# Score matmuls of a cross attention on 128 rows instead of 97 and 98, in a one-core decoder layer

## The reference, cut to what matters

```python
x = x + L0_attn(layernorm(x), ...)              # two Mamba-2 scans, forward and backward
x = x + L0_xattn(layernorm(x), ctx, ctx, ...)   # the part that is changed
x = x + L0_ffn(layernorm(x), ...)               # attention over a mixture of experts

def L0_xattn(q, k, v, padding_mask, ...):       # B, S, D = 4, 1024, 512; 16 heads of HD = 32
    Q, K, V = q @ W_q.T + b_q, k @ W_k.T + b_k, v @ W_v.T + b_v      # split into heads
    scores = einsum('bhqd,bhkd->bhqk', Q, K) / sqrt(HD)
    scores = where(causal, -inf, scores)                # key later than query
    scores = where(padding_mask, -inf, scores)
    return (softmax(scores) @ V) @ W_o.T + b_o
```

## Time and profile before

| | us |
|---|---|
| median of 3 runs | 7218.32 (7214.54 to 7227.69) |
| the profiled execution | 7219.6 |
| its span, first to last instruction | 7217.7 |
| PE busy | 5176.3 (72%) |
| DVE busy | 3053.4 (42%) |
| ACT busy | 1409.7 (20%) |
| POOL busy | 1340.0 (19%) |

### The profile page before, as it was taken

How to read it: one execution, slowest core, us unless ns; L and a number is a source line. 1 busy time by engine, 2 the same in 40 slices (tenths; PEclk the granted TensorE clock), 3 DMA queues, 4 the chain that set the end, 5 groups by cost and what they waited for, 6 DMA issues and landing times. The chain is left out here.

```text
span 7217.7 us, 76090 instructions
## 1 busy us (share of the span) xinstructions
PE 5176.3 (72%) x25256; PEld 3663.9 (51%) x25256; DVE 3053.4 (42%) x6335; ACT 1409.7 (20%) x3256; POOL 1340.0 (19%) x983
## 2 busy tenths in 40 slices
PE   4776666756666766756667678788787859797978
PEld 3555545545445454555455443444435427576666
DVE  3434434434344444444444443343433435344353
ACT  1221212212111211212112123132231310101000
POOL 1222222212214423423424200000000000000000
PEclk8887888877877877877778778888788879788888
DMA  1000000000100000000000231412313120101000
GB/s 49 11 11 8 8 13 7 11 12 7 55 9 20 23 14 12 29 8 17 24 8 21 83 80 35 122 43 75 80 43 113 43 84 6 36 0 36 9 27 21
DMA packets 114630, 236.68 MB, mean 33 GB/s; under 512 B 20373, under 2 KB 20377, under 8 KB 113177
## 3 DMA queue, kind: packets, MB, share of 16 engines
q1 hardware_dynamic: 114200, 231.23, 10.5%
HBM read 155.15 MB, written 67.11 MB: 31 GB/s over the span
## 5 line engine op out<-in xcount | busy, mean ns | idle before, releaser
L1259 DVE TENSOR_REDUCE xa_mx<-xa_s 128x1 f32<-128x128 f32 (+7 forms) x512 | 374.1, 754 | 477.6 <-PE xa_s L1328 471.4
L1172 ACT ACTIVATE xa_src<-xa_gen 128x512 f32<-128x512 f32 (+3 forms) x768 | 354.9, 490 | 600.4 <-PE xa_gen L1348 394.1
L812 PE MATMUL mb_ib<-mb_wc,mb_yT 128*128 128x512 f32 x512 | 280.0, 709 | 225.6 <-ACT mb_yT L529 225.6
L1327 PE MATMUL xa_s<-xa_ka,xa_qa 97*128 97x512 f32 (+3 forms) x768 | 289.6, 442 | 205.2 <-DVE xa_mx L1259 124.6
L812 PE MATMUL mf_ib<-mf_wc,mf_yT 128*128 128x512 f32 x512 | 268.1, 684 | 205.9 <-ACT mf_yT L529 205.9
L1345 PE MATMUL xa_gen<-xa_qa,xa_ka 98*128 98x512 f32 (+3 forms) x768 | 339.4, 466 | 86.4 <-DMA xa_qa<-xa_rows 43.7
L1135 POOL TENSOR_TENSOR xa_res<-xa_res,xa_bor 128x512 f32<-128x512 f32 x32 | 40.3, 1264 | 1769.8 <-DMA xa_res<-after_mamba_dram 1769.8
L72 PE MATMUL ff_gen<-ff_w_hi,ff_st_hi 128*128 128x512 f32 x768 | 309.3, 403 | 0.0
L73 PE MATMUL ff_gen<-ff_w_hi,ff_st_lo 128*128 128x512 f32 x768 | 306.4, 399 | 0.0
L74 PE MATMUL ff_gen<-ff_w_lo,ff_st_hi 128*128 128x512 f32 x768 | 306.2, 399 | 0.0
L622 DVE SCALAR_TENSOR_TENSOR mb_cv<-mb_xc,mb_cw,mb_cv 128x256 f32<-128x256 f32 x432 | 195.6, 526 | 256.0 <-POOL mb_cv L410 254.8
(11 more groups left out here) (441 smaller groups left out, 12948.5 us busy)
## 6 DMA issues: line engine op xcount, KB each, us to landing
xa_qa<-xa_q_dram SPq DMA_DIRECT2D x192, 128.0 KB, 3.2
xa_ka<-xa_k_dram SPq DMA_DIRECT2D x192, 128.0 KB, 3.4
xa_k_dram<-xa_kq SPq DMA_DIRECT2D x32, 512.0 KB, 2.8
xa_q_dram<-xa_kq SPq DMA_DIRECT2D x32, 512.0 KB, 2.8
ff_src<-after_attn_dram SPq DMA_DIRECT2D x64, 256.0 KB, 2.7
mf_xg<-in_x_dram SPq DMA_DIRECT2D x16, 512.0 KB, 3.7
part_dram<-mf_hb SPq DMA_DIRECT2D x32, 256.0 KB, 2.1
mb_xg<-in_x_dram SPq DMA_DIRECT2D x16, 512.0 KB, 3.8
```

The lines of the kernel that those rows point to most:

```text
L812: last = mm(ps[:], yT[:, k, :], wc[:, k, :], start=k == 0, stop=k == KI - 1)
L1172: a_.activation(pe_x[:, s % 2, hh, 0:w], gen["p2", g, s, hh][:, 0:w], ACT.Exp, scale=XSCALE)\
L1259: v_.tensor_reduce(mx[:, g % 2, i, hh:hh + 1], s1[g, hh, i][:, 0:(i + 1) * P], AX.X, ALU.max)\
L1327: mm(ps[:, a:b], qa[s][0:ROW_MAX, i * P:(i + 1) * P], ka[s][0:ROW_MAX, a:b], start=True, stop=b < n)
```

## The change

Every slot tile gets zeros in partitions 96 to 127 at the start, and a row of zeros (`zrow`, a row of the tile `rows`) is made. Both score matmuls then read all 128 partitions. The first pass must not see the maximum that an earlier head left in partition 97 of `qa`, so each head's load also moves `zrow` there, and PE waits for eight transfers instead of seven. The start values take two steps on DVE, zeros and then ones, `const_dve` counts to 2, and SP waits for it ahead of its loop.

```diff
@@ cross_attention
-        mrow, maskf = rows_[0:HG, :], rows_[XD:XD + 1, :]
+        mrow, maskf, zrow = rows_[0:HG, :], rows_[XD:XD + 1, :], rows_[2 * XD:2 * XD + 1, :]
...
-        rows_loaded = [sig(f"rows_loaded{i}", 7 * XH // SLOTS, 16) for i in range(SLOTS)]
+        rows_loaded = [sig(f"rows_loaded{i}", 8 * XH // SLOTS, 16) for i in range(SLOTS)]
@@ sync
             sp.wait_ge(half_ready, 3)
+            sp.wait_ge(const_dve, 2)
             with sp.Fori(0, B) as it:
@@ sync, load(h)
                     sp.dma_start(ka[s][ROW_MASK:ROW_MASK + 1, :].bitcast(F32), maskf.bitcast(F32))\
                         .then_inc(rows_loaded[s].sem, 16)
+                    sp.dma_start(qa[s][ROW_MAX:ROW_MAX + 1, :].bitcast(F32), zrow.bitcast(F32)).then_inc(rows_loaded[s].sem, 16)
@@ vector
             v_.memset(ones[:], 1.0)
+            v_.memset(zrow.bitcast(F32), 0.0)
+            for t in qa + ka:
+                last = v_.memset(t[ROW_MASK:P, :].bitcast(F32), 0.0)
+            last.then_inc(const_dve, 1)
+            dve.wait_ge(const_dve, 1)
             for t in qa + ka:
                 last = v_.memset(t[ROW_MASK:ROW_MAX + 1, :].bitcast(F32), 1.0)
             last.then_inc(const_dve, 1)
-            dve.wait_ge(const_dve, 1)
+            dve.wait_ge(const_dve, 2)
@@ tensor
-            pe.wait_ge(const_dve, 1)
+            pe.wait_ge(const_dve, 2)
@@ tensor, pass1
-                        pe.wait_ge(rows_loaded[s].sem, rows_loaded[s].at(it, 7 * (h // SLOTS) + 6))
+                        pe.wait_ge(rows_loaded[s].sem, rows_loaded[s].at(it, 8 * (h // SLOTS) + 7))
...
-                        mm(ps[:, a:b], qa[s][0:ROW_MAX, i * P:(i + 1) * P], ka[s][0:ROW_MAX, a:b], start=True, stop=b < n)
+                        mm(ps[:, a:b], qa[s][:, i * P:(i + 1) * P], ka[s][:, a:b], start=True, stop=b < n)
@@ tensor, pass2
-                    last = mm(ps[:, 0:n], ka[sl][0:ROW_MAX + 1, j * P:(j + 1) * P], qa[sl][0:ROW_MAX + 1, a:a + n],
+                    last = mm(ps[:, 0:n], ka[sl][:, j * P:(j + 1) * P], qa[sl][:, a:a + n],
                               start=True, stop=not diagonal)
```

## The result

The changed kernel takes 7244.45 us in the median of 10 runs (7226.51 to 7255.08), the kernel before 7221.48 (7209.33 to 7227.89) beside it. The ratio is 1.0032 with a 95% interval of 1.0022 to 1.0042: slower, by 23 us (16 to 30), which is 0.3%. The forecast was 7236, 18 us slower. Ratios here leave out one execution, of the second pass padded, that took 9336 us at a mean clock of 0.54.

The account below looks back on a forecast made before the run. A chain of PE work and DMA waits in cross attention was taken as the bound, PE full at low clock being lost time. Terms 24 + 14 - 20 = +18 us on 7218.3 gave 7236 us, range 7212 to 7262.

Parts of the forecast that it names:

- Start values: Start of cross attention: 17 memsets, a wait and SP's no longer hidden context load delay PE by 24.1 us, bounds 20 to 36.
- the other two bounds: Time of one wide start memset on DVE if not 0.91 us: 0.72 by partitions times columns, or 1.63 if both added up.
- Zero rows: SP's queue: 64 added 4 KB transfers delay the maxima rows and slot releases, costing 14 us, bounds 8 and 18.
- The clock: Second passes of cross attention: padded score matmuls bring the higher granted clock sooner, gaining 20 us, bounds 0 and 80.
- the eight long stretches: Low clock for about 16 us each after head loads of groups 2 and 3; gain 0.6 us each, 5 us together.
- single ones: Single low-clock stretches with a full PE, worth 1.3 us each; four counted on, 5 us.
- No clock gain: Rival: the grant goes by a busy PE, or by rows holding more than zeros; costs of 38 remain, 7256 us; chance 0.20.
- its second form: Variant of the no clock gain rival: only rows that hold more than zeros count towards the granted clock.
- The clock up throughout: Rival: clock stays up through the second pass, removing 154 us of low clock, worth 62 to 69; about 7190 us; chance 0.10.
- Its condition of 95 us of low clock: Removed low clock from which that rival decides: costs of 38 us divided by a worth of 0.4.
- Weight loads ahead: Rival: padding lets the mask matmul's weight loads start early, up to 0.10 us in 1024 pairs; 7161 us; chance 0.06.
- Costs paid back in full: Rival: zero rows cost only 8 us and the clock gains 32, so no change; chance 0.06.

Follow-up runs that it names:

- three moved lines: Kernel before with only the order changed: group 0's maxima rows issued behind the loads of heads 4 and 5 instead of 4 to 7; ratio 0.9961.

## Why the prediction was right

**Start values** (forecast 24.1): 24.1 in the trace after and in the kernel with these alone. The memset on 32 partitions takes 0.91 us; the other two bounds fall.

**Zero rows** (forecast 14, as 2.3 a batch ahead of the maxima, 1.7 at the slots, less 2): 14.6 by the waits of the kernel with these alone. Ahead of the maxima the step was too small: 11.8 / 4 = 2.95 a batch (in the kernel after PE waits 13.6 us in the mean, where 12 to 13 were named). A row costs SP 0.63 and not 0.57, which makes 2.5 for four, and nothing caught up; the other 0.4 is as much as the two profiles of the kernel before differ. At the slots it was too large, 2.8 us in twelve waits and 1.0 in the kernel after, where 6.8 were counted, and kernels without the row lie between 77.4 and 81.0 there, so even 82.0 is hardly a cost. The DMA issues of the kernel after (count, KB, median us to landing), against the earlier trace rows:

```profile
xa_qa<-xa_rows SPq DMA_DIRECT2D x128, 4.0 KB, 2.4
xa_ka<-xa_rows SPq DMA_DIRECT2D x64, 4.0 KB, 2.8
```

The first line mixes the 64 zero rows (median 2.6 us) with the 64 maxima rows (1.8, as before). The mask row, last of a head load before, landed 3.4 us after its issue; now it takes 2.8, and the zero row, issued 0.55 us later, lands only some 0.3 us after it. That the engines were still busy with the head's data, which a later row then waits for less, fits; no run tests it alone.

**The clock** (forecast 20): 17 by the ratio of the padding alone (10 to 23). That it came so near is partly luck, for two errors cancel. Behind the maxima, 46.1 us of low clock became 23.7, much as forecast (46 to 20). But low clock elsewhere went too: the eight long stretches lost 3.4 us each and one of them 6.8, not 1.5, and single ones vanished. In all 302 us became 221 in the kernel after, 80 less where the steps' terms come to about 50. And a low microsecond was worth less: (256.4 - 251.6) x 4 = 19 us for 80, or 0.24, not 0.4. The zero rows' cost is in that too; the padding alone has (256.4 - 250.5) x 4 = 24 us for 88, or 0.27. The 91% busy stretch behind the maxima, from which I took the worth, isn't typical: over the whole second passes PE is busy for 80% (206.24 of 256.68 us in batch 1). Where the clock now rises inside a long stretch, PE waits for DVE. The first pass standing alone, for which the sum has no term, also lost low clock (29.5 us a batch to 24.7 after, to 22.6 in the padding alone, where it got 0.9 us shorter).

**Sum**: forecast +18, measured +23 (16 to 30). The parts measured alone give 28 + 14 - 17 = 25.

**The rivals.** No clock gain falls by the padding alone; its second form, that zero rows don't count, falls by it too, and the ones do no better. The clock up throughout falls: 55 of 252 us are still at 0.50 in each batch's second passes. Its condition of 95 us of low clock was nearly met (80), but the worth of each was 0.24. Weight loads ahead falls; the timeline after, against the earlier trace rows:

```profile
4324.61 0.15 PEld L1355 LDWEIGHTS xa_gen<-xa_later_k,xa_ident_b 128*128 128x128 bf16 x1 [0.20 <-issue]
4324.62 0.33 PE L1355 MATMUL xa_gen<-xa_later_k,xa_ident_b 128*128 128x128 bf16 x1
```

The mask's weight load still starts 0.01 us ahead or less, as in all 512 pairs of the second passes. Costs paid back in full falls by the interval, which starts at 1.0022.

## What to carry to other kernels

A matmul on fewer rows than 128 is no cheaper here, and it keeps the granted clock low for longer after a pause; filling its rows is worth trying where PE stands full at 0.50. Its gain comes only where no other engine or queue is the next limit: here it was a quarter of the low clock removed. What the filling costs at the start and in the queues can be more than that, so it has to come free: zeros written by an idle engine, no transfer per use. And before tuning the clock, look at what stands in the queue ahead of the transfer that everything waits for: three moved lines gave 28 us (19 to 37), the padding 17 (10 to 23).

## What the runs showed of the hardware

- The granted clock depends on the rows that a matmul names. Behind the maxima, with PE full, 97 and 98 rows stayed at 0.50 for 11.0 to 11.9 us in eight stretches of the kernel before, 128 rows for 4.2 to 6.6 in twelve, with zeros or with ones in one operand's added rows. With 112 rows it was 10.7 to 11.9, with one of two alternating passes padded 8.3 to 11.8. In the first pass standing alone, 112 rows did as 128 (21.8 and 22.6 us at 0.50, unpadded 29.5). The Trainium skill (TensorE: Matmul & The Clock Gate, "Part 1: The HAM clock gate") says that the clock goes by how busy PE has been; these runs agree on the two levels and disagree with busy time as the whole measure.
- Less low clock isn't less time by its size: 80 us removed gave 19, 88 gave 24, in passes where PE also waits for DVE.
- A DVE memset of 1024 columns takes 0.91 us on 1, 2 or 32 partitions.
- One program's clock pattern differs between executions in a stage that no edit touches: 317.65 and 326.84 us for the same batch.
